# GpSimd's combine products moved behind the squares of slots 6 and 7, and a last attention step with an order of its own

## What is computed

```python
x = x + attn(layernorm(x)); x = x + moe(layernorm(x))
# attn, 16 heads: queries, keys (16 wide) and values (64 wide) are scaled to length 1
attn = square(relu(q @ k.T)); aggr = attn @ v
out = tanh_norm(aggr) * tanh(silu(gates)); y = out @ Wout
# moe: sigmoid gate, the best 2 of 4 groups, the best 4 of their experts, weights to a sum of 2.5
inter = silu(x @ w_gate[e]) * (x @ w_up[e])
y = sum_e combine[:, e] * (inter @ w_down[e]) + shared expert
```

## Time and profile before

| | |
|---|---|
| median of 3 runs | 663.0 us (662.9 to 663.34) |
| the profiled execution: its own time | 662.09 us |
| its span, first to last instruction | 660.4 us |
| TensorE busy (matmuls) | 635.7 us, 96% |
| VectorE, ScalarE, GpSimd busy | 452.2, 435.4, 439.5 us |
| mean granted TensorE clock | 0.992 |

### The profile page before, as it was taken

How to read it: one execution, slowest core, us unless ns; L and a number is a source line. 1 busy time by engine, 2 the same in 40 slices (tenths; PEclk the granted TensorE clock), 3 DMA queues, 4 the chain that set the end, 5 groups by cost and what they waited for, 6 DMA issues and landing times.

```text
span 660.4 us, 15374 instructions
## 1 busy us (share of the span) xinstructions
PE 635.7 (96%) x5112; PEld 498.1 (75%) x5112; DVE 452.2 (68%) x1693; ACT 435.4 (66%) x1003; POOL 439.5 (67%) x445
## 2 busy tenths in 40 slices
PE   8799999799999999999999999999999999988997
PEld 6666668578787878778787877878787877766787
DVE  6666876385767768576776857676785866656665
ACT  6788876567576866756676675767767576645423
POOL 6858664748677675856767585775768667585632
PEclk9899999799999999999999999999999999999999
DMA  5058999944968959595985959499594949703000
GB/s 172 13 153 190 125 150 133 153 66 117 129 108 134 131 116 111 137 113 105 145 131 107 110 136 125 94 144 138 110 108 127 115 93 151 121 0 83 1 9 16
DMA packets 72557, 72.99 MB, mean 111 GB/s; under 512 B 9408, under 2 KB 70432, under 8 KB 70688
## 3 DMA queue, kind: packets, MB, share of 16 engines
q1 hardware_dynamic: 72480, 72.03, 67.0%
HBM read 53.95 MB, written 18.06 MB: 109 GB/s over the span
## 4 chain that ended last, share of the span: by engine, by line
PE 83%; DVE 5%; ACT 4%; DMA 3%; issue 3%; POOL 2%; SPq 0%; DVEq 0%; POOLq 0%; ACTq 0%
PE ps_a L737 18%; PE ps_f L531 12%; PE ps_f L532 10%; PE ps_f L533 9%; PE ps_f L650 9%; PE ps_f L623 8%; PE ps_s L697 6%; PE ps_f L583 3%; PE ps_f L608 2%; PE ps_f L588 1%; DMA c_rows<-ctr 1%; PE ps_f L632 1%; DMA cb<-c_rows 1%; POOL p L459 1%; DMA big<-in_L_attn_Wkv 1%
## 5 line engine op out<-in xcount | busy, mean ns | idle before, releaser
L459 POOL TENSOR_TENSOR p<-r 128x512 f32<-128x512 f32 x256 | 262.5, 1046 | 151.5 <-ACT r L778 116.2
L778 ACT ACTIVATE r<-ps_s 128x512 f32<-128x512 f32 x256 | 140.3, 609 | 49.8 <-PE ps_s L697 43.3
L737 PE MATMUL ps_a<-p,v 128*64 128x256 f32 x1024 | 146.3, 395 | 8.4 <-POOL p L459 6.3
L737 PEld LDWEIGHTS ps_a<-p,v 128*64 128x64 f32 x1024 | 65.3, 137 | 48.7 <-issue 6.4
L511 POOL TENSOR_TENSOR it<-it,cb 128x512 f32<-128x512 f32 x56 | 71.1, 1281 | 35.1 <-DMA cb<-c_rows 35.1
L1205 DVE TENSOR_TENSOR big<-ps_a,big 128x256 f32<-128x256 f32 x128 | 54.2, 424 | 51.7 <-ACT big L871 49.4
L1158 DVE TENSOR_TENSOR it<-ps_f,it 128x256 f32<-128x256 f32 x130 | 54.8, 421 | 33.8 <-ACT it L852 33.6
L852 ACT ACTIVATE it<-ps_f 128x256 f32<-128x256 f32 x135 | 52.4, 388 | 34.8 <-PE ps_f L533 31.6
L822 ACT ACTIVATE big<-ps_f 128x512 f32<-128x512 f32 x64 | 38.3, 601 | 49.8 <-PE ps_f L533 49.7
L479 POOL TENSOR_TENSOR v<-v,vs 128x512 f32<-128x512 f32 x64 | 67.0, 1057 | 0.2 <-DVE vs L1064 0.2
L650 PE MATMUL ps_f<-wdown,it 128*128 128x128 f32 x504 | 61.8, 277 | 0.9 <-POOL it L511 0.9
(11 more groups left out here) (179 smaller groups left out, 1444.4 us busy)
## 6 DMA issues: line engine op xcount, KB each, us to landing
qk_rows<-qk_parts SPq DMA_DIRECT2D x15, 1024.0 KB, 4.6
qkt<-qk_rows SPq DMA_DIRECT2D x56, 256.0 KB, 9.9
qkt<-qk_rows SPq DMA_DIRECT2D x112, 128.0 KB, 9.3
cb<-c_rows SPq DMA_DIRECT2D x28, 512.0 KB, 5.7
x_in<-in_L_attn_tokens SPq DMA_DIRECT2D x16, 128.0 KB, 6.1
qkt<-qk_rows SPq DMA_DIRECT2D x32, 64.0 KB, 3.0
x_res<-in_L_attn_tokens SPq DMA_DIRECT2D x16, 128.0 KB, 8.7
out<-o_sb SPq DMA_DIRECT2D x16, 128.0 KB, 8.2
```

The lines of the kernel that those rows point to most:

```text
L459: pool.tensor_tensor(p[h % 4][:], r[h % 2][:], r[h % 2][:], ALU.mult).then_inc(probs_done, 1)
L737: last = pe.matmul(ps_a[64 * e:64 * e + 64, 0:N], v[s % 3][:, t, h * DV:(h + 1) * DV], p[h % 4][:, t * N:(t + 1) * N], start=(t == 0), sto ...
L778: act.activation(r[h % 2][:], ps_s[h % 2][:], ACT.Relu).then_inc(relu_done, 1)
```

## The change

1. GpSimd's combine products: none in slot 5; product 0 in slot 6, behind the squares of heads 12 and 13 and `rstd2`; products 1, 2 and 3 in slot 7, behind the squares of heads 14 and 15. This holds for all steps.
2. The down projection waits at chunks 0, 2, 4 and 6 for the product that covers it, not at chunk 0 for all four.
3. Step 15 gets a list of its own: "y2" 0 behind "ones", "rT" ahead of "gu" 3, "cD" and "gu" 4 in slot 4, "gu" 5 in slot 5. VectorE's `gate_up` calls follow (1 and 2 ahead of the routing, 4 in slot 4, 5 in slot 5).
4. "lg" waits for the copy to `x2t` alone, by a semaphore of its own.

```diff
@@ ENDS
+        B - 1: [
+            [("F", "lg", 0), ("N", "ones", 0), ("D", "y2", 0)], [("N", "nT", 0), ("D", "y2", 1)],
+            [("F", "gu", 0), ("F", "gu", 1), ("F", "gu", 2)], [("O", "rT", 0), ("F", "gu", 3), ("O", "rB", 0), ("O", "rB", 1)],
+            [("F", "cD", 0), ("F", "gu", 4), ("O", "rB", 2), ("O", "rB", 3)], [("F", "gu", 5), ("O", "y", 0), ("O", "y", 1)],
+            [("F", "gu", 6), ("F", "gu", 7)], [("F", "gu", 8), ("O", "x2T", 0), SKIP],
+        ],
@@ semaphores
-        ln2_ready, x2h_ready = sem("ln2_ready"), sem("x2h_ready")
+        ln2_ready, x2t_ready, x2h_ready = sem("ln2_ready"), sem("x2t_ready"), sem("x2h_ready")
@@ GpSimd, step
-                    if "F" in on and at < B and k in (5, 6, 7):
+                    if "F" in on and at < B and k in (6, 7):
                         b = s - 2
-                        for j in (((0, 1), (2,), (3,)) if at < B - 2 else ((0, 1), (), (2, 3)))[k - 5]:
+                        for j in ((0,), (1, 2, 3))[k - 6]:
@@ TensorE, filler
                 elif kind == "lg":
-                    pe.wait_ge(x2h_ready, b + 1)
+                    pe.wait_ge(x2t_ready, b + 1)
...
                         if b < BY_DMA:
-                            if c == 0:
-                                pe.wait_ge(it_scaled, 4 * b + 4)
+                            if c < EC and c % 2 == 0:
+                                pe.wait_ge(it_scaled, 4 * b + c // 2 + 1)
@@ ScalarE, evacuate
-                    act.activation(x2t, ps[:, 0:N], ACT.Copy)
+                    act.activation(x2t, ps[:, 0:N], ACT.Copy).then_inc(x2t_ready, 1)
@@ VectorE, step
                         if F:
-                            gate_up([1])
+                            gate_up([1, 2] if at == B - 1 else [1])
                             route_experts(link_f, fb)
                             link_f.end()
+                        if F and at < B - 1:
                             gate_up([2])
...
-                        if F:
+                        if F and at < B - 1:
                             gate_up([4])
...
                         if F:
-                            gate_up([5])
+                            gate_up([4] if at == B - 1 else [5])
...
+                        if at == B - 1:
+                            gate_up([5])
                         if O:
                             dve.wait_ge(x_back[pq], (b - pq) * 8 + 16)
                             residual_row(0)
```

## The result

The changed kernel takes **651.91 us** (median of 4 runs, 650.96 to 652.48) against 663.17 us of the kernel before, run beside it (662.9 to 666.12). The ratio is 0.9846 with a 95% interval from 0.9809 to 0.9883, so it is faster by 11.3 us. Forecast were 651.6 us and a range from 649.5 to 655.4. Five later runs gave 651.91 us once more (650.87 to 652.6) and a ratio of 0.9842 (0.9816 to 0.9869); the kernel before took 662.04 us beside them, so there the gain is 10.1 us. The profiled execution of the changed kernel took 652.48 us, its span is 650.8 us.

A forecast was written before the change was run, and what follows sets the result against it. PE bounds regular steps (busy 37.95 of 38 us), so only less PE work or shorter PE waits help. 6.8 + 1.6 + 3.0 = 11.4 us off 662.09 gives 650.7, plus 0.9 for the median: 651.6 us, range 649.5 to 655.4.

The forecast's parts named there:

- Step 2: Slot 6's squares no longer behind the `cb` wait: 7.1 us loss goes, 0.3 wait at the down projection, gain 6.8 us.
- So this just fits: Step 2, slot 7: second square ends at 120.9, PE wants it at 120.97; a margin of 0.1 us.
- Steps 3 to 13: PE's waits at slot 6's values in four steps go: gain 1.6 us, lower bound 0.5, upper 1.8.
- Steps 14 and 15: Less PE work beside the same POOL work; 1.0 - 0.5 + 0.4 + 2.1 gives 3.0 us, bounds nothing and 6.1.
- Slots 3 to 5: Step 15: four short PE waits cost 2.2 us in starts; the new list leaves 0.1.
- Border: Between steps 14 and 15: the wait for the last product goes, slot 0's squares and "ones" cost some; 0.4 us gained.
- the values end 0.75 after the last [square], at S + 8.0: Slot 7's values in steps 14 and 15; S is the start of the scores of slot 6's heads.
- The rest costs nothing: Down projection's four waits cost 0 to 0.1 us a step; "lg" waiting for `x2t` alone 0, at most 0.3.
- (a): Rival: steps 14 and 15 give nothing, POOL's chain of squares and products setting their pace; 654.6 us, chance 0.12.
- (b): Rival: step 2's stall moves to slot 7 if `cb` lands 2.5 us later; 655.0 us, chance 0.08.
- (c): Rival: slower, three products ahead of the next step's slot 0 squares; 671.1 us at 1.5 a step, chance 0.04.
- (d): Rival: the change does not do what it says, POOL still waits ahead of the squares; 663 us, chance 0.03.

The follow-up runs named there:

- experiment 8: Kernel before with the new product places and the down projection waiting piece by piece, but step 15's old list: 654.11 us, ratio 0.9886.
- experiment 6: Changed kernel with one useless GpSimd product more at the end of slot 7 in steps 2 to 14: 656.6 us, ratio 0.9913.
- experiment 10: Changed kernel with SyncE holding back step 2's load of `cb` until the scores of head 13 are done: 656.66 us, ratio 0.9922.
- experiment 1: Kernel before with only the combine products moved; the down projection still waits at its first chunk for all four: 670.51 us, ratio 1.0137.
- experiment 2: Changed kernel, but the down projection waits at its first chunk for all four products: 665.37 us, ratio 1.006.
- experiment 5: Kernel before with only the waits changed: down projection piece by piece, router for `x2t` alone: 660.91 us, ratio 0.9985.
- experiment 7: Changed kernel with two useless GpSimd products more at the end of slot 7 in steps 2 to 14: 674.37 us, ratio 1.018.
- experiment 3: Changed kernel, but in step 2 alone the products stand in their old places: 658.64 us, ratio 0.9959.
- experiment 4: Changed kernel with the old product places and the down projection's old wait, keeping step 15's list and the router's wait: 661.78 us, ratio 1.0005.

## Why the prediction was right, point by point

**Step 2: right in place and price, wrong in the margin.** The prediction gave 7.1 us for the loss and kept 0.3 for product 3; the trace gives 7.14 and no wait at the down projection. The 0.3 did not come because in this execution `cb` was there 0.2 us before the scores of slot 7, where the earlier trace rows had it 1.24 us behind them; with `cb` 1.4 and 1.5 us behind, the down projection did lose 0.2 (experiments 8 and 6). "So this just fits" was wrong by the step named below: with `cb` 1.24 us behind, the margin of 1.05 gives a loss of 0.2 at the values of slot 7 as well (my estimate from the table of experiment 10). How much step 2 has to lose is not the same in every execution (last section), so the 6.8 of the sum holds for executions like the profiled one.

**Steps 3 to 13: right.** 1.6 forecast, 1.62 measured, and all regular steps now have 3.96 or 3.97 us between the scores of slot 7 and the next.

**Steps 14 and 15: 3.0 forecast, 2.45 measured.** Slots 3 to 5: 2.1 against 2.03 (13.81 to 11.78 us from the scores in slot 1 to the output projection). Border: 0.4 against 0.5 (0.9 gained up to the scores, 0.4 lost at the values of slot 0). The step that was mis-sized is "the values end 0.75 after the last [square], at S + 8.0": they end 1.1 after it, at S + 8.3, because PE starts up to 0.1 us behind the square and six matmuls that start after a stand take 1.0 us to the next start, not 0.75. That is 0.3 in each step, and the whole miss. The same term is in the margin of step 2, where the second square was to be wanted 0.25 us after the first. The upper bound, 6.1, is a slip: its four terms add up to 6.2. A remark behind it: VectorE's operation of L936 did not delay `rstd2` in either step; POOL computed it directly behind the squares. The operation had run 0.1 us ahead of these squares, for 0.17 us each time (its line is now L942). The rule of the Trainium skill, SBUF — State Buffer, section "Who interferes with whom", from which I had estimated a loss of 0.4, was not put to the test in these two steps. In the trace of before every run of it that took longer than 0.17 us lay beside an operation of GpSimd, which agrees.

**"The rest costs nothing": right**, but it hid the most important thing in the change. Experiments 1, 2 and 5 show that the waits piece by piece cost nothing and bring nothing measurable alone, and that without them the move loses 8 us (experiment 1) instead of gaining 8 (experiment 8). My working used them tacitly, by counting with chunk 6 for product 3.

**The rivals.** (a), steps 14 and 15 give nothing: false, 2.45. (b), the stall moves to slot 7: it does not show in the two profiles of the changed kernel (`cb` 0.2 us, and at least 0.5 us, ahead of the scores of slot 7), cost 0.6 and 0.7 us in two executions of experiments 8 and 6, and 2.3 us when the transfer was held back (experiment 10). (c), slower by the squares of slot 0: its mechanism is real, its margin is 1.09 us and was forecast as "0.7 or more" (experiments 6 and 7); two products more would have made the kernel 1.8% slower than the one before. (d): false.

**How near, and how much of it is luck.** 651.6 us forecast, 651.91 measured. The sum was 11.4 us and the two traces give 11.21, but the parts miss by 0.3 us more in step 2 and 0.55 less in steps 14 and 15, and these nearly cancel. The 7.1 us of step 2 is the loss of one execution; two other executions with the old places lost 3.5 (last section), and beside the later groups of the kernel before the changed one gains some 10 us, not 11. That the forecast came within 0.3 us is partly luck; the places and most of the prices are not.

## What to carry to other kernels

In an in-order queue, a job that waits for a transfer stalls everything written behind it; put it behind the work that the bound engine needs next, and then look at who consumes the delayed job: a wait for all of it must become a wait for each part, or the stall comes back there, multiplied by the steps. A stand of the bound engine must be priced from the trace as the distance between starts, since the half clock behind it can cost as much as the stand (experiment 1: 2.14 us of stand, 2.8 us by the clock). Measure a margin by adding work of known size until it costs something.

## What the runs showed of the hardware that was not expected

**The clock does not fall after each stand.** The old places of the products in step 2 were profiled four times. During the stands of 4.36 us (kernel before) and 3.96 us (experiment 3) the clock fell to half, and the distance of the scores was 11.1 us. The stands of 2.60 and 2.55 us (experiments 4 and 5) were followed by full clock, and it was 7.5 us. Experiment 4, PE and two stretches:

```profile
120.02 0.62 PE L743 MATMUL ps_a<-p,v 128*64 128x256 f32 x2 [2.60 <-POOL p L465]
```
```profile
120.00:121.00 1.00, 0.69 (x4) 0.26 (x6) 0.00 (x0) 0.60 (x2) 1.00 (x2) 1.00 1.04 345
121.00:122.00 1.00, 1.00 (x7) 0.46 (x7) 0.35 (x2) 0.50 (x1) 1.00 (x2) 1.00 0.50 165
```

Yet shorter stands elsewhere were enough. In experiment 1 the clock fell during one of 2.14 us, with other short stands just before it (the values of slot 7, twice 0.3 us). In step 15 of experiment 4, the same execution, full clock held for 1.2 us behind the stand of 2.44 us, and then came half clock. A stand of 2.11 us in experiment 7 (values of slot 0, step 15) cost no clock. So the length of one stand does not decide alone.

**The scatter is more than the stall.** The kernel before, in three groups of 10 to 22 runs, spans 656.0 to 665.06 us; the changed kernel, in nine runs of two groups, 650.87 to 652.6. The length of the stand follows when `cb` lands against PE's place: product 0 started 1.24 and 0.84 us after the scores of slot 7 in the two long cases, and 0.6 us before them in the two short ones. That explains 3.6 us between executions (distances of 11.1 and 7.5). It is not the whole scatter: experiment 3, with the old places in step 2, keeps within 2.7 us in ten runs, where ten runs of the kernel before span 4.4, and experiment 8, with the new places, spans 4.1 in four. The half clock at the start of the kernel, which cost 1.3 us more in the first profile of the changed kernel than in that of before, is a second part; what the rest is stays open.
